# Own-token value products moved to four quarters of the matmul array, with their outputs in two banks

## The reference, cut to what matters

```python
q, k, v = x @ Wq.T, x @ Wk.T, x @ Wv.T     # 8 query heads, 4 key/value groups of 64
q, k = rope(rms(q)), rope(rms(k))          # positions kv_len .. kv_len + 63
k_blocks[..], v_blocks[..] = k, v          # written into the paged cache
scores = q . k_all / 16                    # of 256 old keys and the item's own 64
scores = where(in the window of 256, scores, -inf)
p = softmax(scores)
o = p . v_all
x = x + o @ Wo.T
```

## Time and profile before

| | before |
|---|---|
| median of the runs | 1006.88 us (3 runs, 1006.56 to 1006.94) |
| profiled execution, first to last instruction | 960.7 us |
| the same execution's device time | not listed |
| median less span | 46.2 us |
| TensorE busy | 931.3 us, 97% of the span |
| VectorE, ScalarE, GpSimd busy | 604.0, 383.8, 512.8 us |
| the chain that ended last | 91% of the span on TensorE |
| L790 in that chain | 7% of the span |
| L795, 512 records | 41.9 us busy, 282 ns mean of one |

### The profile page before, as it was taken

One profiled execution on the slowest core, in us unless ns is written; L12 is line 12 of the kernel. 1 busy time (PEld: TensorE's weight loads), 2 busy tenths in 40 slices (PEclk: granted clock), 3 DMA queues, 4 the chain that ended last, 5 costly groups with the idle time before them and its releaser, 6 DMA issues.

```text
span 960.7 us, 22134 instructions
## 1 busy us (share of the span) xinstructions
PE 931.3 (97%) x6253; PEld 687.7 (72%) x6253; DVE 604.0 (63%) x1788; ACT 383.8 (40%) x1061; POOL 512.8 (53%) x469
## 2 busy tenths in 40 slices
PE   6899999999999999999997899999999999999997
PEld 4566767667676666767666678877878788878785
DVE  5434344666565644346554777778777787777874
ACT  2121212212122121221223656666666666666662
POOL 1245454544536467664566666555666556565530
PEclk9999999999999999999999999999999999999999
DMA  9888887786776868777734666666666666666741
GB/s 300 272 279 289 292 299 233 262 279 229 257 244 235 279 215 272 233 240 277 265 131 140 192 197 179 192 211 179 201 193 184 211 215 191 197 191 204 220 124 46
DMA packets 105162, 212.48 MB, mean 221 GB/s; under 512 B 29563, under 2 KB 52056, under 8 KB 96930
## 3 DMA queue, kind: packets, MB, share of 16 engines
q1 hardware_dynamic: 71042, 145.54, 45.1%
q0 software_dynamic: 25088, 57.74, 20.5%
q10 hardware_dynamic: 8992, 8.73, 2.8%
HBM read 204.39 MB, written 33.86 MB: 248 GB/s over the span
## 4 chain that ended last, share of the span: by engine, by line
PE 91%; SPq 3%; DMA 2%; issue 1%; DVE 1%; ACT 1%; POOL 0%; DVEq 0%; POOLq 0%; ACTq 0%
PE banks L587 11%; PE banks L802 9%; PE banks L705 9%; PE banks L753 8%; PE banks L790 7%; PE banks L626 6%; PE banks L634 6%; PE banks L636 6%; PE banks L776 6%; PE banks L795 4%; PE banks L730 4%; PE banks L838 3%; PE banks L695 3%; PE banks L710 3%; PE banks L597 2%; PE banks L770 1%
## 5 line engine op out<-in xcount | busy, mean ns | idle before, releaser
L546 POOL DMA_INDIRECT ring<-new_rows,idx x128 | 129.4, 1011 | 82.2 <-DVE big L1278 55.5
L458 POOL TENSOR_TENSOR rms<-ss,neg_half 128x12 f32<-128x12 f32 x31 | 70.8, 2284 | 165.3 <-DVE ss L1184 165.3
L930 ACT ACTIVATE big<-big,neg_max 128x320 f32<-128x320 f32 x256 | 141.3, 555 | 4.2 <-DVE neg_max L1242 4.0
L1242 DVE CUSTOM_DVE_ANT_0 big<-banks,mask 128x320 f32<-128x320 f32 x256 | 114.6, 485 | 32.8 <-PE banks L753 30.7
L587 PE MATMUL banks<-ring 128*64 128x512 f32 x512 | 118.8, 607 | 2.0 <-DMA ring<-in_w 2.0
L871 ACT ACTIVATE x2t_hi<-banks 128x512 fp32r<-128x512 f32 x32 | 19.1, 598 | 235.5 <-PE banks L597 235.5
L920 ACT ACTIVATE kt<-banks 128x384 f32<-128x384 f32 x128 | 62.0, 485 | 95.6 <-PE banks L731 95.5
L587 PEld LDWEIGHTS banks<-ring 128*64 128x64 f32 x512 | 34.6, 138 | 81.6 <-issue 80.4
L535 POOL DMA_INDIRECT ring<-new_rows,idx x64 | 61.5, 961 | 53.2 <-PE banks L776 48.7
L753 PE MATMUL banks<-kt,q_in 64*128 64x128 f32 (+2 forms) x768 | 86.8, 358 | 1.3 <-ACT kt L920 1.3
L1278 DVE TENSOR_SCALAR big<-big,recip 128x320 f32<-128x320 f32 x256 | 86.0, 398 | 2.3
(11 more groups left out here) (169 smaller groups left out, 1980.8 us busy)
## 6 DMA issues: line engine op xcount, KB each, us to landing
ring<-in_w SPq DMA_DIRECT2D x62, 1024.0 KB, 6.0
ring<-in_xt SPq DMA_DIRECT2D x32, 256.0 KB, 2.7
x_in<-in_x SPq DMA_DIRECT2D x32, 256.0 KB, 5.4
bias_in<-in_b SPq DMA_DIRECT2D x64, 128.0 KB, 5.4
x_dram<-x SPq DMA_DIRECT2D x32, 256.0 KB, 5.0
q_dram<-q_t ACTq DMA_DIRECT2D x32, 256.0 KB, 2.3
new_rows<-kv_out SPq DMA_DIRECT2D x32, 256.0 KB, 4.8
q_in<-q_dram SPq DMA_DIRECT2D x64, 128.0 KB
```

What stands on the lines that cost most here:

```text
L546: pool.indirect_dma_start(out=kv[:, s, c, :], out_offset=None, in_=new_rows, in_offset=bass.IndirectOffsetOnAxis(ap=idx[:, b, 1 + c:2 + c] ...
L930: nc.scalar.activation(prob[:, s % 2, g * NK:(g + 1) * NK], sm[:, s % 2, g, :], ACT.Exp, bias=neg_max[:, s % 2, g:g + 1], scale=-1.0, accu ...
L1242: V.tensor_tensor_reduce(sm[:, s % 2, g, :], ps_s[g], mask[:, s % 2, k0:k0 + NK], 1.0, 3.0e38, ALU.add, ALU.min, accum_out=neg_max[:, s % ...
```

## The change

The groups of the second pair change places: group 3 stands first (window, own) and group 2 second (own, window), by a table `PLACE`. Scores, masks, exponentials and normalisations follow it with their offsets. So the own tokens of group 2 (q = 0) come to stand in partitions 64 to 127 and those of group 3 (q = 1) in 0 to 63, and the four matmuls of L795 take row half 0 with column half 0, row half 1 with column half 0, row half 1 with column half 1, and row half 0 with column half 1, in this order. The outputs of pair p go to the first 128 columns of bank 4 + p, in which the transposed probabilities of that pair stood. L967 and L1230 read both banks through one view. The wait for ot_ready moves from ahead of the own-token transposes to behind them, and a second wait for the same count ahead of the value products is gone.

```diff
+PLACE = (0, 1, 3, 2)
...
-        ps_o = ps[6][:, GP * P:2 * GP * P]
+        ps_o = [ps[4 + p][:, 0:P] for p in range(GP)]
+        o_view = banks[:, 4 * BANK:6 * BANK].rearrange("p (g n) -> p g n", g=GP)[:, :, 0:P].rearrange("p g (c t) -> p g c t", t=T)
...
-                        r0, k0 = HD * (g % 2), T * (1 - g % 2)
+                        r0, k0 = HD * (g % 2), T * (1 - PLACE[g] % 2)
...
                     pe.wait_ge(prob_ready, G * b)
                     wait(pe, pt2_ready, b - 1)
-                    wait(pe, ot_ready, b - 1)
                     for p in range(GP):
                         last = nc.tensor.transpose(ps_pt2[:, p * P:(p + 1) * P], prob[:, r % 2, (5 * p + 2) * P:(5 * p + 3) * P], ident[:, :])
                     last.then_inc(pt_done, 1)
+                    wait(pe, ot_ready, b - 1)
...
-                    wait(pe, ot_ready, b - 1)
                     for p in range(GP):
                         for c in range(2):
                             for q in range(2):
                                 v0 = G * HD + (2 * p + q) * HD
-                                nc.tensor.matmul(ps_o[HD * q:HD * q + HD, p * P:(p + 1) * P], kv[:, r, c, v0:v0 + HD], pt[:, p, q, c, :],
-                                                 start=(c == 0 and p == 0), stop=False, skip_group_check=True)
-                    for p in range(GP):
-                        for q in range(2):
-                            v0 = G * HD + (2 * p + q) * HD
-                            last = nc.tensor.matmul(ps_o[HD * q:HD * q + HD, p * P:(p + 1) * P], kv[T * q:T * q + T, r, 2, v0:v0 + HD],
-                                                    pt2[T * q:T * q + T, p, :], start=False, stop=(p == GP - 1), skip_group_check=True)
+                                nc.tensor.matmul(ps_o[p][HD * q:HD * q + HD, :], kv[:, r, c, v0:v0 + HD], pt[:, p, PLACE[2 * p + q] % 2, c, :],
+                                                 start=(c == 0), stop=False, skip_group_check=True)
+                    for q in range(2):
+                        for p in range(GP):
+                            v0, e = G * HD + (2 * p + q) * HD, PLACE[2 * p + q] % 2
+                            last = nc.tensor.matmul(ps_o[p][HD * q:HD * q + HD, :], kv[T * e:T * e + T, r, 2, v0:v0 + HD],
+                                                    pt2[T * e:T * e + T, p, :], start=False, stop=True, skip_group_check=True)
...
-                    nc.scalar.activation(prob[:, s % 2, g * NK:(g + 1) * NK], sm[:, s % 2, g, :], ACT.Exp, bias=neg_max[:, s % 2, g:g + 1],
+                    nc.scalar.activation(prob[:, s % 2, PLACE[g] * NK:(PLACE[g] + 1) * NK], sm[:, s % 2, g, :], ACT.Exp, bias=neg_max[:, s % 2, g:g + 1],
...
-                    nc.scalar.activation(ot_hi[:, ((s - 1) % 4) // 2, :, T * h:T * h + T],
-                                         ps_o[:, 0:2 * P].rearrange("p (c t) -> p c t", c=2 * GP), ACT.Copy).then_inc(othi_ready, 1)
+                    nc.scalar.activation(ot_hi[:, ((s - 1) % 4) // 2, :, T * h:T * h + T].rearrange("p (g c) t -> p g c t", g=GP),
+                                         o_view, ACT.Copy).then_inc(othi_ready, 1)
...
-                    V.tensor_tensor(ot_lo[:, t, :, T * h:T * h + T], ps_o[:, 0:2 * P].rearrange("p (c t) -> p c t", c=2 * GP),
-                                    ot_hi[:, t, :, T * h:T * h + T].bitcast(F32), ALU.subtract).then_inc(ot_ready, 1)
+                    o_lo, o_hi = (o[:, t, :, T * h:T * h + T].rearrange("p (g c) t -> p g c t", g=GP) for o in (ot_lo, ot_hi))
+                    V.tensor_tensor(o_lo, o_view, o_hi.bitcast(F32), ALU.subtract).then_inc(ot_ready, 1)
...
-                    k0 = T * (1 - g % 2)
+                    k0 = T * (1 - PLACE[g] % 2)
```

More of the change, by code:

```diff
@@ L1277, in phase_two @@
                     for g in range(G):
-                        V.tensor_scalar(prob[:, s % 2, g * NK:(g + 1) * NK], prob[:, s % 2, g * NK:(g + 1) * NK], recip[:, s % 2, g:g + 1], None,
-                                        ALU.mult).then_inc(prob_ready, 1)
+                        own_row = prob[:, s % 2, PLACE[g] * NK:(PLACE[g] + 1) * NK]
+                        V.tensor_scalar(own_row, own_row, recip[:, s % 2, g:g + 1], None, ALU.mult).then_inc(prob_ready, 1)
                 if on(b, -1, NB):
```

## The result

The changed kernel takes 995.3 us (median of 4 runs, 993.04 to 999.45); the kernel before, run beside it on the same chip, 1006.74 us (4 runs). The ratio is 0.9891 [0.9864, 0.9917]: 11.4 us faster. The forecast was 994.4 us. Its profiled run took 993.04 us, with a span of 991.2 us; so only 1.8 us lie around the span, not the 46.2 us that the prediction worked with.

The account below looks back on a forecast made before the run. TensorE, busy throughout the second phase's loop, was taken to bound the kernel. 60 x 0.20 = 12.0 us plus 0.5 from the moved wait gave 960.7 - 12.5 + 46.2 = 994.4 us, range 991 to 1003 us.

Parts of the forecast that it names:

- Edit 1: Four own-token value matmuls (L795) in four array quarters: two rounds instead of four, 0.20 us per item, 12.0 us in all.
- A: Rival at the four matmuls: short look-ahead, three rounds instead of four, 999.8 us; chance 0.13.
- B: Rival at the four matmuls: two at a time as before, only the moved wait remains, 1006.4 us; chance 0.09.
- D: Rival at the four matmuls: neighbours sharing an array side shut each other out, slower, 1013 to 1033 us; chance 0.09.
- Edit 2: Outputs to banks 4 and 5, ot_ready wait moved behind the own-token transposes: 0.5 us gained in ramp and tail together.
- Edits 3 and 4: Copy and split over two banks (bounds nothing to 0.80 us); scores, masks, exponentials, normalisations at other offsets: nothing for each.
- Rival C: On odd items VectorE's split or ScalarE's key copy runs late and takes gain back: 997 to 1005 us; chance 0.07.
- The sum: Whole kernel: span 960.7 us less 12.5 us gain plus 46.2 us taken as untouched time above the span, 994.4 us.
- Two items take about 12.88 us: Sign in the second phase's loop: the period of two items falls to 12.88 us from 13.28.
- TensorE stays busy throughout the loop: Sign in the second phase's loop: TensorE shows no idle time; idle ahead of the scores would mean Rival C.

Follow-up runs that it names:

- e3: Changed kernel with only the order of the four matmuls altered, first group pair's two, then the second's; 997.36 us, ratio 0.9923 to the kernel before.
- after: The changed kernel with all its gathers; 995.3 us, ratio 0.9891 to the kernel before.
- few gathers: Kernel before and changed kernel, each with GpSimd's indirect gathers for the first eight items only; 968.22 and 956.81 us.
- second profile of before: The kernel before, unchanged, profiled again; 1003.51 us (one run), span 1001.7 us.
- the three comparisons: The changed kernel, unchanged, against the kernel before in three sets of runs; ratios 0.9891, 0.9896 and 0.9914.
- e4: The kernel before with GpSimd's indirect gathers for the first eight items only; 968.22 us, ratio 0.961 to the kernel before.
- e5: The changed kernel with GpSimd's indirect gathers for the first eight items only; 956.81 us, ratio 0.9496 to the kernel before.
- a0: The changed kernel, unchanged, timed again beside the kernel before; 994.43 us, ratio 0.9896.
- first profile of before: The kernel before, unchanged, in the profile that the prediction worked from; span 960.7 us, while the median of the runs was 1006.88 us.
- e6: Changed kernel with gathers for the first eight items only, as many old and own bytes for the others loaded by SyncE's plain transfers; 957.84 us, 0.9514.
- e7: The changed kernel with each item's third gather issued early, without its wait for the normalisations; 1032.62 us, ratio 1.0234 to the kernel before.
- e8: The changed kernel with each item's third gather issued late, after all scores of the next item; 1016.78 us, ratio 1.0073 to the kernel before.

## Why the prediction was right, and where it was wrong

**Edit 1, the four corners: right in size and mechanism.** The piece is 0.38 us, the windows count four and then eight, and without the late counts an item is 0.20 us shorter. The forecast for the loop, 60 x 0.20 = 12.0 us, stands beside 421.2 - 408.9 = 12.3 us of the scores' stretch without gathers. With that A (three rounds), B (two at a time) and D (a shared side of the array shuts out) are out; e3's other order gives D no hold either. Two rules of the Trainium skill were weighed there. By the Trainium skill, TensorEngine Tiling (Array Packing), Gotcha 1: PSUM Pressure, different row tiles can't access one bank at the same time; the x4 of the first window, by the code, puts both row halves into each of two banks, so for halves that differ in columns too the measurement decides against it. By the Trainium skill, TensorE: Matmul & The Clock Gate, Part 3: Packing small matmuls, matmuls start strictly in program order. If the two halves of a matmul stand side by side in that order, as I took it, L796 would have kept five rounds, and 0.38 us has room for two; but no view here shows in which order the halves stand, so this doesn't decide against the rule.

**Edit 2, the moved wait: small as forecast (0.5 us), and half a miss in what it would show.** The changed layout without corners gives 1.0 us with an interval from 4.2 us faster to 0.4 us slower, so the size can't be told. The tail of after, VectorE's timeline and then TensorE's (start us, us, instruction, idle before):

```profile
976.08 1.27 DVE L1280 TENSOR_SCALAR big<-big,recip 128x320 f32<-128x320 f32 x4
977.27 0.42 DVE L1232 TENSOR_TENSOR ot_lo<-banks,ot_hi 128x256 fp32r<-128x256 f32 x1
```

```profile
977.41 0.44 PE L771 MATMUL banks<-ident,big 128*128 128x128 f32 x2 [1.03 <-DVE big L1280]
977.74 1.09 PE L778 MATMUL banks<-ident,big 128*128 128x128 f32 x8
```

The eight transposes start 0.05 us behind the split's end (977.27 + 0.42 = 977.69), where they stood 947.10 - 946.71 = 0.39 behind it in the earlier trace rows: 0.34 us won, 0.25 forecast. But the idle time stands, as before, ahead of the two own-token transposes, which now wait for the last normalisation; I had put it ahead of the eight. The two, started earlier, fill the gap that I had left there.

**Edits 3 and 4: nothing, right.** L968 and L1232 have the 0.38 and 0.42 us of the earlier trace rows, and with few gathers an item is shorter by all of edit 1's 0.20 us. **Rival C**, that another engine takes the gain on the odd items, isn't seen: with few gathers TensorE waits for no engine.

**The sum: the step that failed.** "The median of the runs, 1006.88 us, lies 46.2 us above the span, which the edit doesn't touch." No such time lies around the span: 1.8 us do, in the second profile of before. The profile on which I worked was an execution without late counts, and the profiled ones among the timed runs have them inside the second phase, in the very loop of which I said that TensorE is never idle. I should have doubted it: a constant of 46.2 us around a program of 960 us had no row behind it. The forecast came out because the late counts cost nearly the same in both kernels, so that a sum against the wrong execution kept the right difference. That was luck: nothing in the prediction gave a reason for it.

**The size of the gain** is 12.5 us in the forecast and 11.4, 10.6 and 9.2 us in the three comparisons; e4 and e5 differ by 11.4. By the mean time of two items, taken by the trace from the tenth L795 (or L796) to the sixtieth, few gathers bring them from 13.27 to 12.87 us, the forecast 0.40; with all gathers they go from 14.62 to 14.27, or to 14.32 in the second run of after (a0): 0.30 to 0.35. Late counts thus add 1.34 us to two items before and 1.40 to 1.45 after: some 0.06 to 0.11 x 32 = 2 to 3.5 us of the gain are given back to them. That agrees with the three comparisons, but their spread from chip to chip is as large, so this is worked out and not shown by a run of its own. "Two items take about 12.88 us" and "TensorE stays busy throughout the loop" came true only where the gathers were gone.

## What to carry to other kernels

Small f32 matmuls that use a quarter of the array can be placed in four different quarters and run together: four of them took 0.38 us instead of 0.58, in both orders tried, and it was the placing of the operands that won; the two banks and the moved wait alone gave 1.0 us, not to be told from nothing. When a profile's span and the timed runs are far apart, take a second profile before you call the rest a constant: here the scores' stretch holds 457.8 - 417.5 = 40.3 of the 1001.7 - 960.7 = 41.0 us between the two profiles. And look at what GpSimd issues when waits end late without a releaser; moving one gather of an item by about a microsecond changed the time by 16 to 32 us.

## What the runs showed of the hardware

While GpSimd issues an indirect gather, and until some 0.6 to 0.75 us after its recorded end (in a few cases 1.2), counts that TensorE raises can arrive late, by 1.14 us in the mean for those due within 0.25 us after such an end in after. Counts of ScalarE and VectorE were not seen late. In this kernel the late counts are worth about 38 us of 1006. That it isn't the gathers as such follows from the first profile of before, which has all its gathers and no late count: two items take 13.28 us there, as they do with few gathers (13.27). The runs exclude the bytes (e6) and the edit (second profile of before), and show that the place of the issues matters (e7, e8).

The late rises fall where the gather's own transfers begin: in after, over the gathers between 560 and 925 us, 1071 packets of the queue that GpSimd fills start 0.60 to 0.65 us behind the end of a gather's instruction, and 308 start 0.50 to 0.55 us behind it. The first profile of before has the same peak (1346 against 311) and no late count, so this alone doesn't do it. What in the gather holds the counts up stays open, and whether the count or the matmul's end is late; and also why one execution, the first profile of before, had 220 such issues in its loop and no late count.
